# Gated attention unit unrolled over four batches, with the next batch's preparation placed inside and behind the score loop

## The reference

```python
def _L0_attn_b_ref(x, ln_w, ln_b, uv_w, uv_b, gamma, beta, w, o_w, o_b):
    shortcut = x
    xn = (x - mu) / jnp.sqrt(var + EPS) * ln_w + ln_b
    uv = jax.nn.silu(xn @ uv_w.T + uv_b)
    u, v, base = (uv[..., :E], uv[..., E:2 * E], uv[..., 2 * E:])     # E = 256, S = 128
    base = _rope(base[:, :, None, :] * gamma[None, None] + beta)
    q, k = (base[:, :, 0, :], base[:, :, 1, :])
    qk = jnp.einsum('bis,bjs->bij', q, k)
    kernel = jnp.square(jax.nn.relu(qk / SQRT_S + bias[None]))
    out = u * jnp.einsum('bij,bje->bie', kernel, v)
    return out @ o_w.T + o_b + shortcut
...
x = x + _L0_attn_b_ref(_layernorm(x, axis=-1), ...)
```

## Time and profile before

| | us |
|---|---|
| median of 3 runs | 3764.24 |
| lowest and highest run | 3761.12, 3766.71 |
| the profiled execution | 3772.41 |
| its span, first to last instruction | 3769.2 |
| PE busy in the span | 2795.5 (74%) |
| DVE busy in the span | 2229.2 (59%) |
| ACT busy in the span | 1601.7 (42%) |
| POOL busy in the span | 707.9 (19%) |

### The profile page before, as it was taken

One profiled execution on the slowest core, in us unless ns is written; L12 is line 12 of the kernel. 1 busy time (PEld: TensorE's weight loads), 2 busy tenths in 40 slices (PEclk: granted clock), 3 DMA queues, 4 the chain that ended last, 5 costly groups with the idle time before them and its releaser, 6 DMA issues.

```text
span 3769.2 us, 55186 instructions
## 1 busy us (share of the span) xinstructions
PE 2795.5 (74%) x18720; PEld 1601.4 (42%) x18720; DVE 2229.2 (59%) x4893; ACT 1601.7 (42%) x2886; POOL 707.9 (19%) x926
## 2 busy tenths in 40 slices
PE   2998899899899926367762636666665688888888
PEld 1666566566566626333332622222222253233225
DVE  2564555455456431355553238889796988777754
ACT  1665566476466502111100314242433333666672
POOL 2000000000000064300016332212121221222221
PEclk9999999999999958688875867778777798999998
DMA  5000000000000011100001210000000034011000
GB/s 157 1 0 2 1 0 1 2 1 0 2 1 0 12 39 52 39 0 0 0 4 39 60 28 0 0 0 0 0 0 0 0 116 157 2 47 47 2 2 23
DMA packets 65897, 78.75 MB, mean 21 GB/s; under 512 B 9005, under 2 KB 41948, under 8 KB 65712
## 3 DMA queue, kind: packets, MB, share of 16 engines
q1 hardware_dynamic: 56816, 60.10, 4.9%
q0 software_dynamic: 8896, 16.29, 1.6%
HBM read 43.58 MB, written 35.52 MB: 21 GB/s over the span
## 4 chain that ended last, share of the span: by engine, by line
PE 28%; DVE 15%; issue 13%; POOL 4%; another core or an unknown queue 3%; ACT 2%; DVEq 0%; DMA 0%; POOLq 0%; SPq 0%; ACTq 0%
DVE Wqkv L1737 4%; PE ps L1613 3%; PE ps L844 3%; PE ps L971 2%; PE ps L590 2%; PE ps L838 2%; PE ps L579 2%; DVE arena L1433 2%; PE ps L1585 1%; DVE arena L1438 1%; POOL arena L1465 1%; PE ps L1574 1%; PE ps L980 1%; POOL slots_in L749 1%
## 5 line engine op out<-in xcount | busy, mean ns | idle before, releaser
L431 DVE CUSTOM_DVE_ANT_0 arena<-ps,causal 128x512 f32<-128x512 f32 (+3 forms) x512 | 282.7, 589 | 345.3 <-PE ps L247 343.8
L355 ACT ACTIVATE arena<-ps 128x512 f32<-128x512 f32 (+1 forms) x640 | 337.8, 548 | 321.7 <-PE ps L260 318.9
L368 ACT ACTIVATE arena<-arena 128x640 f32<-128x640 f32 (+7 forms) x512 | 393.8, 770 | 36.7 <-DVE arena L431 32.7
L1737 DVE TENSOR_REDUCE Wqkv<-ps 128x2 f32<-128x1024 f32 (+3 forms) x384 | 353.3, 953 | 87.1 <-PE ps L1578 81.7
L260 PE MATMUL ps<-ident,arena 128*128 128x128 f32 x2304 | 359.5, 283 | 46.1 <-ACT arena L368 44.6
L1693 ACT ACTIVATE arena<-ps 128x1024 f32<-128x1024 f32 (+3 forms) x384 | 302.3, 809 | 163.0 <-PE ps L1585 159.3
L281 PE MATMUL ps<-arena,rope 128*64 128x128 f32 x4608 | 350.5, 282 | 0.0
L1433 DVE TENSOR_TENSOR_SCAN arena<-arena 128x1024 f32<-128x1024 f32 x128 | 318.9, 2532 | 9.2 <-ACT arena L1379 4.7
L260 PEld LDWEIGHTS ps<-ident,arena 128*128 128x128 f32 x2304 | 249.0, 141 | 177.0 <-issue 144.2
L1308 PE MATMUL ps<-arena,ident 128*128 128x512 f32 x512 | 281.7, 702 | 0.0
L281 PEld LDWEIGHTS ps<-arena,rope 128*64 128x64 f32 x4608 | 242.3, 136 | 74.8 <-issue 64.1
(11 more groups left out here) (259 smaller groups left out, 4824.0 us busy)
## 6 DMA issues: line engine op xcount, KB each, us to landing
arena<-q_dram SPq DMA_DIRECT2D x4, 2048.0 KB, 8.8
arena<-k_dram SPq DMA_DIRECT2D x4, 2048.0 KB, 14.1
q_dram<-arena SPq DMA_DIRECT2D x24, 256.0 KB, 3.7
k_dram<-arena SPq DMA_DIRECT2D x24, 256.0 KB, 3.8
arena<-slots_in SPq DMA_DIRECT2D x8, 640.0 KB, 4.5
slots_out<-arena SPq DMA_DIRECT2D x8, 640.0 KB, 3.9
slots_in<-arena POOLq DMA_DIRECT2D x4, 640.0 KB, 7.9
W<-in_m_W_dram SPq DMA_DIRECT2D x1, 2048.0 KB, 9.9
```

Of the source, the lines that this page charges most:

```text
L355: nc.scalar.activation(k.probT[:, n % 2, b0 * P:(b0 + nb) * P], k.ps[:, 4 + m % 2, 0:nb * P], ACT.Copy)\
L368: nc.scalar.activation(k.prob[:, i % 2, h, 0:w], k.prob[:, i % 2, h, 0:w], ACT.Exp, bias=k.neg_max[:, i % 2, h:h + 1], scale=-1.0, accum_o ...
L431: ins = nc.vector.tensor_tensor_reduce(k.prob[:, i % 2, h, 512 * g:512 * g + w], k.ps[:, banks[h], 0:w], k.causal[:, first:first + w], 1.0 ...
L1737: nc.vector.tensor_reduce(k.least[:, g, a, i % 4, c, :], k.ps[:, 2 * (m % 3):2 * (m % 3) + 2, 0:search_width(i, c)], AX_X, ALU.min)\
```

## The change

The hardware loop over the batches is gone. `pe_gau`, `act_gau`, `dve_gau` and `pool_gau` are now each called once, and go over the four batches in the code, with semaphores that count on from batch to batch (and one `finish(5)` at the end instead of four). Inside:

- DVE's normalisation is cut into 14 pieces (`dve_norm_piece`). The pieces of batch b+1 stand in batch b's score loop, one behind each half u. Pieces 3 and 9 are empty: there POOL works out the root. Those of batch 0 stand ahead of everything.
- PE transposes the tokens of b+1 between the last two `mix` steps of b, and computes base, u and the rotated base of b+1 behind the last `mix`, then the results of b, then v of b+1.
- The output weights' results go to banks 2 and 3, four tiles to a bank, and DVE adds them in two instructions of 512 columns, placed behind `gq` and `gk` of b+1 and ahead of v's bias.
- ACT makes the first two affine copies ahead of the Silu of u.
- DVE computes `gq` and `gk` ahead of v's bias, and waits for the affine copies one at a time. Its wait for its own `kern` at each u is gone.

The diff's core:

```diff
+def dve_norm_piece(nc, k, dve, ch, sm, b, piece, out):
+
+    if piece in (0, 1, 6, 7):
+        for t in range(4 * (piece % 2), 4 * (piece % 2) + 4):
+            last = nc.vector.bn_stats(k.bn6[:, t, :], (k.X_all[:, 8 * b + t, :] if piece < 2 else k.XN[:, t, :]))
+        ch.link(last)
+    elif piece in (2, 8):
...
+    elif piece in (4, 5, 10, 11):
+        dve.wait_ge(sm[("rstd1", "rstd2")[piece // 10]], b + 1)
...
 def pe_gau(nc, k, pe, sm):
...
+    def base(b):
+        pe.wait_ge(sm["xnT"], 2 * b + 2)
+        if b >= 1:
+            pe.wait_ge(sm["biased"], 16 * b)
...
+    def gate(b):
+        for c in range(2):
+            if b >= 1:
+                pe.wait_ge(sm["gated"], 4 * b - 1 + c)
...
+    def mix(b, j):
+        if j == 0:
+            pe.wait_ge(sm["v"], b + 1)
...
+    def results(b):
+        pe.wait_ge(sm["gated"], 4 * b + 4)
+        pe.wait_ge(sm["biased"], 16 * b + 16)
...
+    for b in range(k.B):
+        for j in range(8):
+            scores(b, j)
+            if j >= 1:
+                mix(b, j - 1)
+        if b + 1 < k.B:
+            pe.wait_ge(sm["biased"], 16 * b + 14)
+            pe_tokens(nc, k, pe, sm, b + 1, k.XN2)
+        mix(b, 7)
+        if b + 1 < k.B:
+            base(b + 1)
+            gate(b + 1)
+            rotated(b + 1)
+        results(b)
+        if b + 1 < k.B:
+            value(b + 1)
...
 def dve_gau(nc, k, dve, ch, sm):
...
+    def prepare(b):
         for c in range(2):
+            dve.wait_ge(sm["affine"], 4 * b + c + 1)
+            ch.mark(nc.vector.tensor_tensor(k.gaff[:, c, :], k.gaff[:, c, :], k.cos[:], ALU.mult))
+        for c, dst in enumerate((k.gq, k.gk)):
+            dve.wait_ge(sm["affine"], 4 * b + 3 + c)
+            ch.link(nc.vector.tensor_tensor(k.gaff[:, 2 + c, :], k.gaff[:, 2 + c, :], k.sin[:], ALU.mult))
+            nc.vector.tensor_tensor(dst[:], k.gaff[:, c, :], k.gaff[:, 2 + c, :], ALU.add).then_inc(sm["qk"], 1)
+        if b >= 1:
+            add_results(b - 1)
+        dve.wait_ge(sm["v_ps"], b + 1)
...
+            if b + 1 < k.B:
+                norm_piece(b + 1, u)
...
-            with pe.Fori(5, 5 + B) as b:
-                use_batch(k, b - 5)
-                pe_gau(nc, k, pe, k.G)
-                finish(b)
+            pe_gau(nc, k, pe, k.G)
+            finish(5)
```

More of the change, by code:

```diff
@@ L794, in sp_moe @@
         sp_results(nc, k, sp, sm, b)
-G_SEMS = LN_SEMS + ["l2_" + n for n in LN_SEMS] + [
-    "base_ps", "base", "rot_ps", "u_ps", "u", "v_ps", "v_sum", "v", "affine", "rot_done", "qk", "s_ps", "biased", "kern",
-    "kv_ps", "gated", "y_ps", "x_new"]
+G_SEMS = ["var1", "rstd1", "var2", "rstd2", "xn2", "xnT_ps", "xnT", "base_ps", "base", "rot_ps", "u_ps", "u", "v_ps",
+          "v_sum", "v", "affine", "rot_done", "qk", "s_ps", "biased", "kern", "kv_ps", "gated", "y_ps", "x_new"]
 def sub(sm, prefix):
@@ new lines, in half @@
+def half(ap, g):
+    return ap[:, g * 512:(g + 1) * 512]
+def dve_norm_piece(nc, k, dve, ch, sm, b, piece, out):
[4 more added lines that the diff above has]
+    elif piece in (2, 8):
+        for t in range(8):
+            last = nc.vector.bn_aggr(k.mv[:, t, :], k.bn6[:, t, :])
+        ch.link(last)
+        nc.vector.tensor_scalar(k.var_eps[:], k.mv[:, :, 1], EPS, None, ALU.add).then_inc(sm[("var1", "var2")[piece // 8]], 1)
+    elif piece in (4, 5, 10, 11):
+        dve.wait_ge(sm[("rstd1", "rstd2")[piece // 10]], b + 1)
+        if piece == 10 and b >= 1:
+            dve.wait_ge(sm["xnT_ps"], 2 * b)
+        for t in range(4 * (piece % 2), 4 * (piece % 2) + 4):
+            src, dst = (k.X_all[:, 8 * b + t, :], k.XN[:, t, :]) if piece < 10 else (k.XN[:, t, :], out[:, t, :])
+            last = nc.vector.tensor_scalar(dst, src, k.mv[:, t, 0:1], k.rstd[:, t:t + 1], ALU.subtract, ALU.mult)
+        if piece < 10:
+            ch.link(last)
+        else:
+            last.then_inc(sm["xn2"], 1)
+    elif piece == 12:
+        X = k.X_all[:, 8 * b:8 * b + 8, :]
+        ch.link(nc.vector.tensor_tensor(X, X, k.XN[:], ALU.add))
@@ new lines, in act_gau @@
+def act_gau(nc, k, act, sm):
+    for b in range(k.B):
+        act_tokens(nc, k, act, sm, b, k.g_cols[:, 0:1], k.g_cols[:, 1:2])
+        act.wait_ge(sm["base_ps"], b + 1)
+        nc.scalar.activation(k.base[:], k.ps[:, 2:4, :].rearrange("p a b -> p (a b)"), ACT.Silu, bias=k.uvb[:, 4:5])\
+            .then_inc(sm["base"], 1)
+        act.wait_ge(sm["base"], b + 1)
+        for c in range(2):
+            nc.scalar.activation(k.gaff[:, c, :], k.base[:], ACT.Identity, scale=k.g_cols[:, 2 + 4 * c:3 + 4 * c],
+                                 bias=k.g_cols[:, 3 + 4 * c:4 + 4 * c]).then_inc(sm["affine"], 1)
+        for c in range(2):
+            act.wait_ge(sm["u_ps"], 2 * b + c + 1)
+            nc.scalar.activation(k.gu[:, c, :], k.ps[:, 4 + 2 * c:6 + 2 * c, :].rearrange("p a b -> p (a b)"), ACT.Silu,
+                                 bias=k.uvb[:, c:c + 1]).then_inc(sm["u"], 1)
+        act.wait_ge(sm["rot_ps"], b + 1)
+        for c in range(2):
+            nc.scalar.activation(k.gaff[:, 2 + c, :], k.ps[:, 0:2, :].rearrange("p a b -> p (a b)"), ACT.Identity,
+                                 scale=k.g_cols[:, 4 + 4 * c:5 + 4 * c], bias=k.g_cols[:, 5 + 4 * c:6 + 4 * c])\
+                .then_inc(sm["affine"], 1)
+        act.wait_ge(sm["v_sum"], 4 * b + 4)
+        nc.scalar.activation(k.gv[:], k.gv[:], ACT.Silu).then_inc(sm["v"], 1)
@@ L2172, in _ @@
                 pe_mamba(nc, k, pe, k.S)
[L2173 removed]
+                finish(b + 7)
             pe_late(nc, k, pe, k.F1, True)
```

239 lines of the change are left out of this document (115 added, 124 removed).

## The result

The changed kernel takes 3667.15 us (median of 4 runs, 3666.39 to 3668.52) against 3764.07 us before (4 runs, 3761.12 to 3766.71). The ratio is 0.9743, with a 95% interval from 0.9726 to 0.9760: 96.9 us less. The forecast was 3670 us, in a range from 3658 to 3706.

What follows compares the result with a forecast made beforehand. PE bounds the score loop, a chain through all engines the rest. The stage's end, 1629.9 + 37.8 + 3 x 59.0 + 8.1 + 0.6 = 1853.4 against 1948.2, gains 94.8 us: 3670 us, range 3658 to 3706.

Steps and rivals of the forecast that it cites:

- Step 1: PE behind the loop: waits 0.5 us for the third `gated`; u ends at 5.7, output weights at 11.9, v at 15.4.
- Steps 2 and 3: ACT's and DVE's work up to the first `mix`: `qk` complete at 14.0 us, v's Silu at 20.2, PE waits 1.4.
- Step 4: Score loop: 5.15 us per block if DVE keeps up, 34.3 us against PE's 41.2; a middle batch costs 59.0 us.
- Step 5: First batch's front, normalisations still in series: `mix(0)` starts at 1629.9 instead of 1637.2, 7.3 us earlier.
- Step 6: Last batch's tail, PE waiting for all four `gated`: 8.1 us instead of 6.7, a loss of 1.4.
- 7.3 - 1.4 us: First batch's front starts `mix(0)` 7.3 us earlier; the last batch's tail loses 1.4 us.
- PE's 2.6 us ahead of the first scores: PE idle before the first batch's scores: a lowered clock could cost between 0 and 2.9 us; 0 was taken.
- The table loads: Silu's table loads, one per turn, go; they lie under PE's base, worth 0 to 1.3 us each; 0 was taken.
- The code loads: Instruction loads of the unrolled stage: some 5 to 6 on PE, about 4 to 5 small ones elsewhere; cost taken as 0.
- DVE as the bound: Rival, 8%: DVE bounds the score loop, each piece costing 0.3 us more, 9 us in all, so 3679 us.
- the stalls on loads: Two rivals on instruction loads: PE's stall as in M2, 3706 to 3710 us (11%); every engine's stall, 3797 us (3%).
- the clock at the short waits: Rival, 4%: the clock falls at PE's short waits for v, 12 us more, so 3682 us.

## Why the prediction was right

**What bounds the kernel.** Right. The loop was and is PE, and DVE's wait of 2.28 us a block was the room: one block's wait is about as long as two pieces. That the wait was the cover is shown by the run with everything in one block and by the doubled pieces.

**Step 1, PE behind the loop.** Right in structure, too dear in one term. PE waits 0.26 us for the third `gated`, not 0.5. The output weights take 3.57 us for 32 records (1671.43 to 1675.00), not 4.5: the 1.13 us for 8 was read at a place where the code makes PE wait, from the third tile on, for DVE's addition of the tile two before, so it was the pace of the pair and not of PE. Run in one go they take 0.11 us a record. The transposes, priced by the same row, took 0.87, not 1.1.

```profile
1671.43 3.73 PE L922 MATMUL ps<-owT,arena 128*128 128x128 f32 x32
...
1675.00 3.62 PE L890 MATMUL ps<-uvT,XNT 128*128 128x256 f32 x16
```

**Steps 2 and 3, the string to the first `mix`.** Right in kind, 0.9 us too long. Counted from the end of the loop at 1664.04 us, `qk` is complete at 13.7 us (14.0 in the forecast), the two additions of the results at 14.9 (15.5), v's bias at 17.3 (18.1) and its Silu at 19.25 (20.2): each link took 0.1 to 0.3 us less, among them the small margins that the forecast had put between them. That the wait for v came out so near, 1.28 us for 1.4, is luck: PE was ready for the first `mix` 0.8 us earlier than forecast, by the cheaper output weights, and v 0.9 us earlier, by the shorter string.

**Step 4, DVE keeps up.** Right. A middle batch takes 58.1 us, 59.0 was forecast. The output weights were also 0.9 us cheaper, but this is not the difference by itself: the first `mix` waited for v, at the end of the string, and PE's time ahead of it ends in the wait. It was a condition, though. PE's records of v end at 1678.62 us and DVE began on their bias at 1678.87, so with output weights 0.9 us longer that bias would have begun some 0.7 us later (an estimate from these two rows), and the batch would have come near the 59.0. The point where DVE would bind lies 5 us of work further; the sum of 34.3 in 41.2 had given 6.9.

**Step 5, the first front.** 34.7 us from the first statistics to the first `mix`, 35.0 forecast. In the other executions of the same front it took 35.4 to 36.5 us, with PE's records at a lower clock, so the 0.3 is within what an execution adds.

**Step 6, the last tail.** 9.2 us up to M2, 8.7 forecast, by two errors of opposite sign. The 32 records were priced at 4.6 us, again by the row of the pair; at full clock they take 3.84 us, as in the repeat of the kernel, whose tail took 7.6 us. In the first result's trace the clock was down and they took 5.47 us. The forecast had no term for the clock here.

The sum had 94.8 us for the stage; it gave 97.1. The front's 0.3 and three times 0.95 for an interval, less 0.5 in the tail and 0.2 in the last loop, is the difference.

**The parts of the gain.** By the twelve runs, added one after another: order inside a batch 20.7 us (hardware loop kept), unrolling 5.6, normalisations under the loop 53.5, projections beside the tail 16.4; together 96.2. The forecast of 7.3 - 1.4 us for the order in a batch, four times 5.9, is 24. The parts hold for this order of adding them. Taken back from the finished kernel, each alone, the two halves of the new order cost 38.3 and 8.2 us, over twice their 20.7 without the overlap.

**Two-sided prices.** PE's 2.6 us ahead of the first scores: 2.29 us were measured, followed by 8 records in 3.70 us, full clock. Taking 0 was right in this trace and luck beyond it: in other executions the same records behind 2.75 us took 5.2 us (last section). The table loads fell from two in each turn (the prediction had counted one) to one in the whole stage, and are not seen in the sum. The code loads: 6 instead of 2, no wait; the prediction had 9 to 11, so that its small loads of the other engines hardly came. The rule of the Trainium skill ("Runtime: NRT & Kernel Launch", Instruction fetch mechanics), that crossing a block is mostly hidden, holds here. That section of the Trainium skill has a taken branch break the prefetch where its target lies outside the two blocks of code at hand. No run here shows that case: the kernel before made only 2 loads for four turns, none of them from 1700 to 1948 us. The sharing of an interface by Pool and DVE instructions of two SBUF inputs, which the Trainium skill states ("Advanced Engine Details and Errata", GPSIMD Details), did no harm that shows: DVE's L1014 takes 692 ns on the mean, as L906 did, and one that ran wholly inside a root of POOL took 0.69 us:

```profile
1642.75 1.64 POOL L842 TENSOR_TENSOR rstd<-var_eps,minus_half 128x8 f32<-128x8 f32 x1 [11.20 <-DVE var_eps L822]
...
1643.30 0.69 DVE L1014 SCALAR_TENSOR_TENSOR arena<-arena 128x512 f32<-128x512 f32 x1
```

**The rivals.** DVE as the bound, the stalls on loads, the clock at the short waits: none of them at work, except the clock in the last tail. The price of the rivals on loads, 10 us each, came from a row read too broadly: of the 36.3 us of idle time at L590 the row gives 22.7 to ACT and 6.8 to DVE, and only 6.8 are without a releaser. With the 14.2 at L579 that is 21 us for 5 loads, some 4 us each. The last section shows that even these do not come with the loads.

## What to carry to other kernels

Where one engine fills a loop and another waits in it, the other's idle time per step is room for the next turn's preparation, if it is spread over the steps: the same 12 us of work were free in 14 pieces and cost 12 us in one. How large a piece may be was not measured beyond that. Ahead of overlapping, put the operations on the string to the loop in front of those that only wait: adding v's bias ahead of gq and gk cost 38 us even in the overlapped kernel. And read an engine's pace only from rows where it did not wait between instructions.

## What the runs showed of the hardware

**The experts' waits do not belong to the code, nor to its loads.** The M2 rows on which two rivals rested came back in the first result's trace (16.6 us at L579 without a releaser) and not in that of the repeat. From M1's first statistics to the end of its combine the changed kernel took 277 us in the first result's trace (from 1313 us on) and 207 in that of its repeat, with the same instructions. Rows of PE's and DVE's waits between 1400 us and the end of M1, the first result and then the repeat (`issue` and `remote`: the trace knows no releaser for the wait):

```profile
DVE arena L714 <- remote: 30.3, 3, 16.0
...
PE ps L579 <- issue: 15.6, 1, 15.6
```

```profile
DVE arena L714 <- PE ps L579: 43.8, 30, 2.7
...
PE ps L579 <- DVE arena L708: 5.2, 3, 3.9
```

The two rows of the repeat stand in the first trace too, with 46.4 and 5.2 us. What the repeat does not have is the other two: no `remote` wait, and no `issue` wait of PE. Instruction loads alone do not make these waits. From the first statistics of M2 to the end of its combine both traces have 5 loads; in the first result's PE has `issue` waits of 23.4 us there and the stretch takes 276 us, in the repeat it has none and takes 208. What makes the waits stays open. It may be the chip: the kernel before took 3764 us in all four runs beside the first result, and 3624 us on each of three other occasions, on three chips (25 runs). But as the first result's chip is not on record, another circumstance of that session is not excluded.

**The clock after a short wait can go either way.** In the last tail PE waits 2.58 us in both traces of the same kernel. The rows of the first and of the second:

```profile
1840.06 5.47 PE L922 MATMUL ps<-owT,arena 128*128 128x128 f32 x32 [2.58 <-DVE arena L1021]
```

```profile
1768.78 3.84 PE L922 MATMUL ps<-owT,arena 128*128 128x128 f32 x32 [2.58 <-DVE arena L1021]
```

The granted clock was 0.70 from 1840.0 to 1845.6 us in the first. The same wait cost 1.6 us in one execution and nothing in the other. It goes so in all traces: of 21 such waits of 2.57 to 2.65 us ahead of the 32 records, 10 are followed by records in 5.3 to 5.5 us and 11 by records in 3.84. Ahead of the first eight score records it is the same, within one execution even, that of the normalisations alone in the loop:

```profile
1614.73 3.70 PE L903 MATMUL ps<-arena 128*128 128x512 f32 x8 [2.29 <-DVE arena L992]
...
1679.11 5.39 PE L903 MATMUL ps<-arena 128*128 128x512 f32 x8 [2.29 <-DVE arena L992]
```

Of 20 such waits of 2.29 to 2.76 us, 6 were followed by records in 5.2 to 6.8 us and 14 by records in 3.70. The changed kernel's waits of 1.28 us ahead of a batch's first `mix` were followed by 3.70 us for 8 records each time, six times in two traces. So a wait of 2.3 to 2.8 us has two prices, 0 or some 1.5 to 3 us, and its length alone does not decide which: 2.29 us and 2.58 us had both. The prediction had both for the first front and took 0; for the tail it should have had both too.
